# A graph layer's SBUF tensors placed in another order: every operand of the loop's matmuls at a multiple of 64 bytes

## The reference

```python
msg_in = concat([x[src], x[dst]], -1)              # 100,000 x 256
h = relu(msg_in @ Wm1 + bm1)                       # 256 -> 256
h = relu(h @ Wm2 + bm2)                            # 256 -> 256
messages = h @ Wm3 + bm3                           # 256 -> 128
agg = segment_sum(messages, dst) / clip(count, 1)
upd = relu(concat([x, agg], -1) @ Wn1 + bn1) @ Wn2 + bn2
return layernorm(x + (x + upd))
```

## The kernel before, in words

| tensor | use in the loop's matmuls | start, modulo 128, before | after |
|---|---|---|---|
| `w2` | moving, L1442 | 0 | 0 |
| `h1` | stationary, L1442 | 32 | 0 |
| `onehot_t` | moving, L1329 | 32 | 0 |
| `b_win` | stationary, L1329 | 32 | 0 |
| `onehot` | stationary, L1346 to L1354 | 32 | 0 |
| `h2_hi`, blocks 0 to 7 | moving, L1346 and L1352 | 32, 40, 48, ... 88 | 0, 64, 0, 64, ... |
| `h2_lo` | moving, L1350 and L1354 | 96 | 0 |
| `ident`, `a_edge` | moving and stationary, L1418 | 32 | 0 |
| `ones2` | stationary, L1452 | 32 | 0 |
| `wc` | stationary, L1483 | 0 | 0 |
| `f_hid`, groups 0, 1, 2, 3, ... (in `agg`) | stationary, L1496 | 0, 32, 64, 96, ... | 32, 64, 96, 0, ... |
| `wn2` | moving, L1496 | 0 | 0 |

## Time and profile before

### The profile page before, as it was taken

One profiled execution on the slowest core, in us unless ns is written; L12 is line 12 of the kernel. 1 busy time (PEld: TensorE's weight loads), 2 busy tenths in 40 slices (PEclk: granted clock), 3 DMA queues, 4 the chain that ended last, 5 costly groups with the idle time before them and its releaser, 6 DMA issues.

```text
span 1200.9 us, 33955 instructions
## 1 busy us (share of the span) xinstructions
PE 1170.1 (97%) x9614; PEld 1149.9 (96%) x9615; DVE 961.7 (80%) x2072; ACT 747.9 (62%) x1392; POOL 770.2 (64%) x814
## 2 busy tenths in 40 slices
PE   6889999999999999999999999999999999999996
PEld 6778999999999999999999999999999999999886
DVE  6775877788788878888888888888888888888676
ACT  3555666666666666666666666666666666664684
POOL 2067777777777777777777777777777777771000
PEclk9998999999999999999999999999999999999999
DMA  9776666666665666666666666566666666662022
GB/s 327 274 289 176 181 179 175 179 181 177 180 178 178 178 180 177 179 177 179 178 179 179 180 178 179 176 180 177 180 179 176 179 180 178 179 177 75 27 71 92
DMA packets 135605, 211.42 MB, mean 176 GB/s; under 512 B 24247, under 2 KB 102669, under 8 KB 134030
## 3 DMA queue, kind: packets, MB, share of 16 engines
q0 software_dynamic: 37536, 102.55, 29.9%
q1 hardware_dynamic: 98030, 108.43, 29.4%
HBM read 188.09 MB, written 22.80 MB: 176 GB/s over the span
## 4 chain that ended last, share of the span: by engine, by line
PE 94%; DVE 1%; SPq 1%; DMA 1%; issue 1%; POOL 0%; ACT 0%; DVEq 0%
PE bank L1442 46%; PE bank L1418 14%; PE bank L1329 8%; PE sums L1352 4%; PE sums L1346 4%; PE sums L1350 4%; PE sums L1354 4%; PE bank L1483 3%; PE sums L1496 2%; PE bank L1239 1%; DMA a_table<-work 1%; PE bank L1466 1%; PE bank L1224 1%; PE sums L1224 1%; PE bank L1479 0%
## 5 line engine op out<-in xcount | busy, mean ns | idle before, releaser
L635 POOL DMA_INDIRECT a_edge<-a_table,src_idx x782 | 750.8, 960 | 258.9 <-issue 155.3
L1442 PE MATMUL bank<-w,h 128*128 128x256 f32 x4692 | 620.8, 282 | 0.0
L1442 PEld LDWEIGHTS bank<-w,h 128*128 128x128 f32 x4692 | 584.5, 189 | 0.0
L737 ACT ACTIVATE h<-bank 128x512 fp32r<-128x512 f32 x391 | 233.9, 598 | 324.7 <-PE bank L1329 321.8
L1111 DVE SCALAR_TENSOR_TENSOR h<-bank,h 128x512 fp32r<-128x512 f32 x391 | 269.4, 689 | 121.7 <-ACT h L737 85.7
L1123 DVE SCALAR_TENSOR_TENSOR h_lo<-bank,h_hi 128x512 fp32r<-128x512 f32 x391 | 266.7, 682 | 0.0
L726 ACT COPY bank<-b_bc 128x512 f32<-128x512 f32 x391 | 231.6, 592 | 42.9 <-DVE h_lo L1123 38.2
L1418 PE MATMUL bank<-ident,a_edge 128*128 128x128 f32 x1564 | 235.4, 273 | 5.7 <-DVE onehot_t L1028 3.9
L745 ACT ACTIVATE h_hi<-bank 128x512 fp32r<-128x512 f32 x391 | 232.9, 596 | 2.9 <-PE bank L1442 2.9
L1028 DVE TENSOR_SCALAR onehot_t<-rel,node_half 128x256 fp32r<-128x256 int16 x391 | 143.8, 368 | 57.8 <-DMA rel<-rel_dram 40.6
L1329 PE MATMUL bank<-onehot_t,b_win 128*128 128x256 f32 x782 | 189.9, 324 | 0.0
(11 more groups left out here) (190 smaller groups left out, 681.9 us busy)
## 6 DMA issues: line engine op xcount, KB each, us to landing
b_win<-b_table SPq DMA_DIRECT2D x391, 128.0 KB
rel<-rel_dram SPq DMA_DIRECT2D x196, 128.0 KB
a_edge<-a_table,src_idx POOLq DMA_INDIRECT x782
a_table<-work SPq DMA_DIRECT2D x12, 512.0 KB, 4.6
b_table<-work SPq DMA_DIRECT2D x5, 1024.0 KB, 6.0
b_table<-h SPq DMA_DIRECT2D x4, 1024.0 KB, 5.1
f_x<-in_x SPq DMA_DIRECT2D x12, 256.0 KB, 4.7
b_table<-a_edge SPq DMA_DIRECT2D x3, 1024.0 KB, 5.9
```

Source lines behind the costliest of these rows:

```text
L635: pool.indirect_dma_start(a_edge[:, b % R * TB + t, :], None, a_table, bass.IndirectOffsetOnAxis(ap=src_idx[:, b * TB + t:b * TB + t + 1], ...
L737: act.activation(h1[:, k % U, 0, :], bank[k % 2][:, :], ACT.Relu).then_inc(s_h1h, 1)
L1442: ins = pe.matmul(to, h1[:, j, a, h * EB + t * P:h * EB + (t + 1) * P], w2[:, b, h, :], start=False, stop=(a == 1 and h == KH - 1), skip_g ...
```

## The change

Three edits. The tensors are placed in another order: those that the loop's matmuls read come first, the odd-sized ones last. `h2_hi`'s blocks grow from 258 to `HP = H + 16 = 272` columns, so that each starts at a multiple of 64 bytes. The two matmuls that read `h2_hi` take its columns 0 to `HC`, 258 as before. The instructions on each engine are the same as before, in the same order and of the same sizes; only addresses differ. `agg` comes to lie 32 bytes past a multiple of 64, where it had lain at one.

```diff
@@ -48,6 +48,7 @@
     HC = H + 2
+    HP = H + 16
@@ -66,36 +67,14 @@
-        f_x = sb("f_x", [P, NW, D], F32)
-        agg = sb("agg", [P, (NW + 1) * HC], F32)
...
         w2 = sb("w2", [P, 2, KH, H], F32R)
+        wc = sb("wc", [P, 2, KH, H], F32R)
         b2_bc = sb("b2_bc", [P, TB, H], F32)
-
+        wn2 = sb("wn2", [P, KH, D], F32)
         b3_rows = sb("b3_rows", [P, H], F32R)
         bn2_rows = sb("bn2_rows", [P, D], F32R)
-        wc = sb("wc", [P, 2, KH, H], F32R)
-        wn2 = sb("wn2", [P, KH, D], F32)
-        bn1_col = sb("bn1_col", [P, KH], F32)
         ones2 = sb("ones2", [P, P], F32R)
         ident = sb("ident", [P, P], F32)
         a_edge = sb("a_edge", [P, R * TB, H], F32)
         rel = sb("rel", [P, RC, 2 * EB], I16)
         b_win = sb("b_win", [P, RB, H], F32R)
@@ -103,13 +82,29 @@
         onehot_t = sb("onehot_t", [P, 3, EB], F32R)
         onehot = sb("onehot", [P, U + 1, TB, P], F32R)
         h1 = sb("h1", [P, U, 2, KH * EB], F32R)
-        h2_hi = sb("h2_hi", [P, U, TB, HC], F32R)
+        h2_hi = sb("h2_hi", [P, U, TB, HP], F32R)
         h2_lo = sb("h2_lo", [P, U, TB, H], F32R)
+        f_x = sb("f_x", [P, NW, D], F32)
+        WORK = 11910
+        work = sb("work", [P, WORK], F32)
+        agg = sb("agg", [P, (NW + 1) * HC], F32)
...
+        bn1_col = sb("bn1_col", [P, KH], F32)
@@ -1343,13 +1338,13 @@
-                return pe.matmul(to[:, 0:HC], onehot[:, slot, 0, :], h2_hi[:, k % U, 0, :], start=start,
+                return pe.matmul(to[:, 0:HC], onehot[:, slot, 0, :], h2_hi[:, k % U, 0, 0:HC], start=start,
                                  stop=False, skip_group_check=True)
...
-                pe.matmul(to[:, 0:HC], onehot[:, slot, 1, :], h2_hi[:, k % U, 1, :], start=False, stop=False,
+                pe.matmul(to[:, 0:HC], onehot[:, slot, 1, :], h2_hi[:, k % U, 1, 0:HC], start=False, stop=False,
                           skip_group_check=True)
```

More of the change, by code:

```diff
@@ L66, in sem @@
             return ctx.enter_context(nc.semaphore(name))
+        w2 = sb("w2", [P, 2, KH, H], F32R)
+        wc = sb("wc", [P, 2, KH, H], F32R)
+        b2_bc = sb("b2_bc", [P, TB, H], F32)
+        wn2 = sb("wn2", [P, KH, D], F32)
+        b3_rows = sb("b3_rows", [P, H], F32R)
+        bn2_rows = sb("bn2_rows", [P, D], F32R)
+        ones2 = sb("ones2", [P, P], F32R)
+        ident = sb("ident", [P, P], F32)
+        a_edge = sb("a_edge", [P, R * TB, H], F32)
+        rel = sb("rel", [P, RC, 2 * EB], I16)
+        b_win = sb("b_win", [P, RB, H], F32R)
+        b_far = sb("b_far", [P, H], F32R)
+        onehot_t = sb("onehot_t", [P, 3, EB], F32R)
+        onehot = sb("onehot", [P, U + 1, TB, P], F32R)
+        h1 = sb("h1", [P, U, 2, KH * EB], F32R)
+        h2_hi = sb("h2_hi", [P, U, TB, HP], F32R)
+        h2_lo = sb("h2_lo", [P, U, TB, H], F32R)
         f_x = sb("f_x", [P, NW, D], F32)
+        WORK = 11910
+        work = sb("work", [P, WORK], F32)
         agg = sb("agg", [P, (NW + 1) * HC], F32)
@@ L86, in gnn_layer @@
         flags_act = sb("flags_act", [1, NI], I32)
[L88 to L92, removed]
-        wc = sb("wc", [P, 2, KH, H], F32R)
-        wn2 = sb("wn2", [P, KH, D], F32)
-        bn1_col = sb("bn1_col", [P, KH], F32)
[L96 to L101, removed]
-        b_far = sb("b_far", [P, H], F32R)
-        onehot_t = sb("onehot_t", [P, 3, EB], F32R)
-        onehot = sb("onehot", [P, U + 1, TB, P], F32R)
-        h1 = sb("h1", [P, U, 2, KH * EB], F32R)
-        h2_hi = sb("h2_hi", [P, U, TB, HC], F32R)
-        h2_lo = sb("h2_lo", [P, U, TB, H], F32R)
+        bn1_col = sb("bn1_col", [P, KH], F32)
         FAR = 2
         FURTHER = U
-        WORK = 11910
-        work = sb("work", [P, WORK], F32)
         bank = [ctx.enter_context(nc.psum_tensor(f"bank{i}", [P, 512], F32)) for i in range(4)]
```

## The result

| | before | changed |
|---|---|---|
| median of 11 runs | 1202.36 us (1200.11 to 1205.51) | 1205.78 us (1203.99 to 1209.4) |
| ratio | 1 | 1.0034, 95% interval 1.0024 to 1.0043 |
| span of the profiled execution | 1200.9 us | 1203.2 us |

What follows compares the result with a forecast made beforehand. PE was taken as the bound, its matmuls' number times their spacing. Order 0, h2_hi's padding -1.3, agg, setup and tail 0: 1202.66 - 1.3 = 1201.4, with the runs' median 0.3 lower, 1201 us; range 1136 to 1213.

Steps and rivals of the forecast that it cites:

- The bound: Whole loop: PE busy 97% of the span; 7038 products each some 9 ns too long, 63 us at stake.
- 64-byte starts: Loop and other float32r products: the excess does not hang on them; aligning the moving operand alone is worth 0 to 2 ns.
- On the reading above the loop's products keep their 118 ns: 0 us.: Order of the tensors, loop products: instructions are the same, so the new order changes nothing, 0 us.
- Rival C: Loop products: streams starting at the same place modulo 128 bytes hinder each other, 120 ns, 1213 us; chance 0.20.
- The objection to C: L1350 and L1354: they stand 64 apart from their stationary operand, like the fast pair, yet have some 120 ns.
- `h2_hi` padded, -1.3 us: L1346 and L1352: padding ends odd starts of h2_hi's blocks, 1.6 ns on 782 products, 1.3 us gained.
- Rival B: PE's products: one unaligned operand brings the whole excess, so aligning both gains up to 63 us and 4 outside, 1135 us; chance 0.38.
- POOL's two gathers need 2.32 us.: POOL, per batch: two gathers with their issue time take 2.32 us, under the 2.40 us batch of rival B's full gain.

Runs made afterwards that it cites:

- shift: The changed kernel with 32 bytes put ahead of its first tile, so every loop operand starts 32 past a multiple of 64: 1206.64 us, 1.0044 of before.
- the map: PE alone, none of the layer computed: 24 float32r products in a row for each pair of start addresses; 256 columns took 113.3 to 120.4 ns each.
- order_only: The kernel before with the new order of the tensors alone, h2_hi's rows left at 258 columns: 1207.18 us, ratio 1.0055.
- pad_only: The kernel before, old order of the tensors kept, with h2_hi's rows padded to 272 columns: 1199.42 us, ratio 0.9984.
- level: The changed kernel with every tile at the same place modulo 256 bytes, h2_hi's rows padded to 320 columns: 1209.45 us, ratio 1.0076.
- apart: The changed kernel with stationary tiles 64 bytes further, modulo 256, than the moving ones, h2_hi's rows padded to 320 columns: 1200.24 us, ratio 0.997.

## Why the prediction was wrong, point by point

- **The bound.** Right: PE bound the kernel before and after, the excess of 9 ns over what a product could take was the only stake, and L1442's spacing was the one to watch: 8 of the 10.6 ns that a batch lost are its.
- **64-byte starts.** Right, and by its own argument: whichever operand was aligned, the rows had the same spacing. `shift` and the map show it for multiples of 32.
- **"On the reading above the loop's products keep their 118 ns: 0 us."** This is the step that failed. From "The same again, whichever operand is aligned" it drew that nothing in the addresses counts, though the earlier trace rows showed 6 ns from an address alone, and it put the order of the tensors at nothing. The order cost 5.7 us by `order_only`, whose loop differs from that of the kernel before in `w2`'s distance (0, not 32) and in 64-byte starts, which `shift` shows to be worth nothing. The same step with the padded `h2_hi`, from `pad_only` at 0.9984 to the changed kernel at 1.0034, costs as much. That one distance is the loss.
- **Rival C** had the sign, and that it hangs on how the two starts lie to each other, with a chance of 0.20; its period of 128 bytes was wrong, and that the streams get in each other's way is argued still. Its price of 7 to 10.6 us belongs to a kernel with distance 0 everywhere, and `level` measures 8.0 us for that one. In the loop `level` differs from the changed kernel in `h2_hi`'s blocks alone, and has L1437 at 120 ns from the second matmul on. The changed kernel, with `h2_hi`'s blocks at 0, 192, 128 and 64, reaches 120 only for the last four to six of the twelve. That left 3.4 us.
- **The objection to C**, that L1350 and L1354 stand 64 apart and have 120 ns, was read wrongly twice. They stand at -64, that is 192, which modulo 256 is not 64. And a single product between others, two of them 258 columns wide, doesn't show the spacing that a run of equal ones settles into: in `apart` all four stand at 64 and still have 120.
- **`h2_hi` padded, -1.3 us.** Measured -1.9 us in the old order, within an interval of 0.2 to 3.5. So the size was near; that is luck as far as the reason goes, the odd start, which is not shown: (8, 8) has the 120.0 of (0, 0) in the map. Padding changes distances too, `h2_lo`'s among them.
- **Rival B** is refuted as it stood: `keep_busy`'s 19 matmuls, now with both operands aligned, took 4.62 us against 4.70, both by their row of the timeline. That small gain is distance 0 at 512 columns, 226.7 ns in the map against 233.3 at 32; `keep_busy` has it for its last eight spacings only. It is far from the 213 that B needed.
- **"POOL's two gathers need 2.32 us."** Wrong by 8%: it averaged the 155 us of "issue" over all gathers. The wait of 0.30 us stands before each gather, hidden where another wait was put down for the same gap. This would have made rival B's 1135 us impossible too: 2.50 us a batch and not 2.40 is 39 us more.

## What to carry to other kernels

Where back-to-back float32r products of 256 columns bound a kernel, ask how the stationary and the moving tiles lie to each other modulo 256 bytes, not how each is aligned. A gap of one small tensor is a cheap trial: here the stationary tile 64 bytes ahead gained up to 5 ns a product, in a run of equal ones, and level was the worst of the three placements tried. At 512 columns level was the best of the map. Before a gain on the bounding engine is priced, count the time per round of the next engine from its starts, its issue gaps included, since that sets what can be kept.

## What the runs showed of the hardware that was not expected

- The spacing of float32r products of 256 columns is between 113.3 and 120.4 ns in the map, at the full granted clock. It depends on the distance of the two operands modulo 256 bytes, and on which steady pattern a run falls into. Float32 transposes stay at 109 ns at distances 0 and 64 alike (the kernel before and `apart`).
- The floor of 113.3 ns is 4 ns above those transposes. No pair of starts got below it at 256 columns. It is also only 1.6 ns above the 111.7 of float32r products with half as many columns, each with a weight load of its own, so that the load may set it; no run tests that. Above the 106.7 ns of 256 columns at 2.4 GHz the floor is 6.7 ns and the 120.0 of distance 0 is 13.3; 512 columns at distance 0 are 13.3 above their 213.3 as well. What the floor consists of stays open, as does what picks one of two steady patterns at distances 64 and 192.
- That the two read streams of PE meet somewhere is argued from the dependence on their distance alone; the runs don't show where, or by what.
